# Windowed attention before a convolution: the probabilities become the stationary operand, and the weighted values are transposed back

## The reference

```python
def _L0_conv_ref(x, ac_w, ac_b, qkv_w, proj_w, proj_b):     # 16 heads of 8 channels, windows 8 x 8
    g = clip((x * ac_w + ac_b) * x, 0.0, 6.0)
    qkv = einsum('bchw,dc->bdhw', g, qkv_w)                   # cut into windows of 64 tokens
    attn = softmax(einsum('wnqd,wnkd->wnqk', q, k) * hd ** -0.5)
    o = einsum('wnqk,wnkd->wnqd', attn, v)
    return einsum('bchw,dc->bdhw', o, proj_w) + proj_b
...
x = x + _L0_conv_ref(_gn(x), ...)
x = x + _L1_conv_ref(_gn(x), ...)                             # 3 x 3 convolution, padding 1, plus bias
```

## Time and profile before

| | |
|---|---|
| median of 3 runs | 1495.81 us (1494.65 to 1499.69) |
| profiled execution: its time, its span | 1495.76 us, 1494.0 us |
| busy share TensorE, VectorE, ScalarE, GpSimd | 78%, 82%, 67%, 42% |
| mean granted clock of TensorE | 0.942 of full |
| DMA: moved, share of the engines' time | 144.93 MB, 29.6% for the kernel's queue |

### The profile page before, as it was taken

How to read it: one execution, slowest core, us unless ns; L and a number is a source line. 1 busy time by engine, 2 the same in 40 slices (tenths; PEclk the granted TensorE clock), 3 DMA queues, 4 the chain that set the end, 5 groups by cost and what they waited for, 6 DMA issues and landing times. The chain is left out here.

```text
span 1494.0 us, 56299 instructions
## 1 busy us (share of the span) xinstructions
PE 1171.3 (78%) x21860; PEld 696.7 (47%) x21860; DVE 1232.3 (82%) x1891; ACT 994.7 (67%) x1683; POOL 620.4 (42%) x438
## 2 busy tenths in 40 slices
PE   1288888988898986878747888988898898768875
PEld 1155555655565654333324555555565565423332
DVE  6678778887887985999985878887887888679998
ACT  2768777877787874544425877877787788644442
POOL 7124333433334432565632333333333334336665
PEclk9989999999999997899987999999999999979999
DMA  6143333333333330032324333333333343101111
GB/s 249 55 124 105 114 106 95 123 107 94 114 115 93 124 106 4 29 112 84 112 98 147 111 116 98 109 113 102 104 115 104 104 125 113 30 0 57 42 56 70
DMA packets 115466, 144.93 MB, mean 97 GB/s; under 512 B 21000, under 2 KB 91048, under 8 KB 114216
## 3 DMA queue, kind: packets, MB, share of 16 engines
q1 hardware_dynamic: 115240, 141.44, 29.6%
HBM read 72.16 MB, written 69.24 MB: 95 GB/s over the span
## 5 line engine op out<-in xcount | busy, mean ns | idle before, releaser
L503 ACT ACTIVATE work<-ps,ws 128x512 f32<-128x512 f32 x512 | 337.1, 682 | 61.8 <-PE ps L972 42.8
L734 DVE TENSOR_REDUCE m_all<-ps 128x8 f32<-128x512 f32 x512 | 328.1, 683 | 45.2 <-PE ps L949 44.0
L409 POOL TENSOR_TENSOR work<-work 128x512 f32<-128x512 f32 x128 | 162.7, 1271 | 370.4 <-ACT work L511 370.4
L415 POOL TENSOR_TENSOR g_lo<-work,g_hi 128x512 f16<-128x512 f32 x128 | 145.6, 1158 | 327.9 <-ACT g_hi L548 327.9
L960 PE MATMUL ps<-q_stack,k_stack 128*64 128x64 f16 x8192 | 216.4, 200 | 25.7 <-DMA q_stack<-max_scratch 24.0
L960 PEld LDWEIGHTS ps<-q_stack,k_stack 128*64 128x64 f16 x8192 | 179.4, 114 | 84.3 <-DMA q_stack<-max_scratch 45.4
L972 PE MATMUL ps<-work,v_ext 128*32 128x64 f32 x8192 | 210.1, 226 | 6.5 <-ACT work L503 0.6
L906 PE MATMUL ps<-work,c_hi 128*128 128x512 f16 x384 | 150.5, 392 | 69.6 <-DVE work L825 69.5
L601 ACT CAST work<-work 128x640 f16<-128x640 f32 x128 | 92.0, 720 | 145.6 <-DVE work L821 99.6
L949 PE MATMUL ps<-k_stack,q_stack 128*64 128x256 f16 x2048 | 177.8, 291 | 13.8 <-issue 4.8
L972 PEld LDWEIGHTS ps<-work,v_ext 128*32 128x32 f32 x8192 | 137.2, 110 | 92.0 <-issue 69.3
(11 more groups left out here) (130 smaller groups left out, 2022.9 us busy)
## 6 DMA issues: line engine op xcount, KB each, us to landing
stack_scratch<-work SPq DMA_DIRECT2D x128, 256.0 KB, 2.1
q_stack<-stack_scratch SPq DMA_DIRECT2D x64, 384.0 KB
k_stack<-stack_scratch SPq DMA_DIRECT2D x256, 96.0 KB
stack_scratch<-work SPq DMA_DIRECT2D x128, 128.0 KB, 2.1
out_dram<-work SPq DMA_DIRECT2D x32, 512.0 KB, 2.7
img<-in_x_dram SPq DMA_DIRECT2D x8, 1024.0 KB, 14.2
img<-in_x_dram SPq DMA_DIRECT2D x16, 512.0 KB, 3.9
q_stack<-zero_scratch SPq DMA_DIRECT2D x64, 32.0 KB
```

Source lines behind the costliest of these rows:

```text
L409: g.tensor_tensor(recip[h], sums[h], guess[h], ALU.mult).then_inc(near_done, 1)
L415: g.tensor_tensor(g_lo[:, m, :, e, :], g32.rearrange("p (w q) -> p w q", w=UW), g_hi[:, m, :, e, :], ALU.subtract).then_inc(g_lo_done, 1)
L503: a.activation(probs[:, w % 2, :], ps[:, ST_B + w % 2, :], ACT.Exp, scale=ws[:, R_EXP:R_EXP + 1]).then_inc(exp_done, 1)
L734: v.tensor_reduce(m_all[:, 0, 2 * h:2 * h + 2, p, :], ps[:, S_B + h, :].rearrange("p (g j k) -> p g j k", g=2, k=WIN), AX.X, ALU.max).then ...
```

## The change

The weighting is turned. `probs` holds a pair of windows (two halves of 512 columns), twice. `weigh(d, md, p)` takes 64 columns of `probs` as stationary operand and streams the 18 columns of `v_ext`: 16 values and 2 sums for a pair of heads. The output has tokens along partitions, so a sum stands beside its values; VectorE takes an ordinary reciprocal of 32 numbers a partition and multiplies with it (`divide`). `turn` transposes the result back on TensorE, `turned` copies it out on ScalarE, and `output` is one product instead of two. The shuffles, the guessed reciprocal and its Newton step fall away, with ScalarE's and GpSimd's part of them.

`g_hi` and `g_lo` are written once. `v_rows` writes the two head parities to the two halves of the partitions in 48 products of 64 columns instead of 24 of 128. The transposed maxima get a bank of their own (M_B) and rows 96 to 103 of `q_stack` are no longer filled with zeros from DRAM, since `scores` reads 96 rows.

The stages are shifted: a new stage E (unit i-1) holds the rest of D, and R works on unit i-2. The order on each engine is new. On TensorE a step is now: scores(0), weigh(n-1, 1), project(0), scores_t(n-1, 2), output(n-2), scores(1), weigh(n-1, 2), project(1), scores_t(n-1, 3), turn(n-1, 0), scores(2), weigh(n-1, 3), scores_t(n, 0), v_rows, scores(3), weigh(n, 0), scores_t(n, 1), turn(n-1, 1), transpose of the maxima. Maxima and exponentials stay one bank each. SyncE sends the maxima first, then q and k.

```diff
-VC = 4 * HD
+VC = 2 * HD + 2
...
-                return {s for s, lead in (("G", 4), ("H", 3), ("B", 2), ("C", 1), ("D", 0), ("R", -1), ("X", -2))
+                return {s for s, lead in (("G", 4), ("H", 3), ("B", 2), ("C", 1), ("D", 0), ("E", -1), ("R", -2))
...
+                    if "D" in on:
+                        after(sp, m_in, n - 1)
+                        after(sp, m_hi_done, n)
+                        after(sp, m_lo_done, n)
+                        sp.dma_start(maxd[m], m_pair[:, :, :]).then_inc(m_sent, 16)
+                        after(sp, m_sent, n)
+                        after(sp, st_done, n - BUFS)
+                        sp.dma_start(q_stack[ROWS:ROWS + MROWS, m, :, :].rearrange("r g (p t) -> r (g p) t", p=PAIRS),
+                                     maxd[m].rearrange("(a j) s t -> (j s) a t", j=HJ)).then_inc(m_in, 16)
                     if "B" in on:
...
+                        write(d, mb, 0)
+                        write(d, mb, 1)
                         after(sp, q_sent, d)
+                        after(sp, st_done, d - BUFS)
                         sp.dma_start(q_stack[0:ROWS, mb, :, :],
...
+                    def exps(d, p):
+
+                        after(act, pv_done, d, p - 1)
+                        for w in range(2):
+                            after(act, st_done, d, 2 * p + w + 1)
+                            a.activation(probs[:, p % 2, 512 * w:512 * w + 512], ps[:, ST_B + w, :], ACT.Exp,
+                                         scale=ws[:, R_EXP:R_EXP + 1]).then_inc(exp_done, 1)
...
+                    def turned(d, h):
+
+                        after(act, ot_done, d, h + 1)
+                        after(act, proj_done, d - 1)
+                        a.copy(o_t[:, 256 * h:256 * h + 256], ps[:, GA, 256 * h:256 * h + 256]).then_inc(ot_out, 1)
...
                     def divide(d, h):
 
...
+                        bank = ps[:, PV_B + h, 0:2 * HP * VC].rearrange("p (a c) -> p a c", c=VC)
+                        after(dve, pv_done, d, 2 * h + 2)
+                        v.reciprocal(rec[h], bank[:, :, 2 * HD:VC]).then_inc(rec_done, 1)
+                        after(dve, rec_done, d, h + 1)
+                        after(dve, ot_done, d - 1, h + 1)
+                        v.tensor_tensor(o_n[h].rearrange("p (a e d) -> p a e d", e=2, d=HD),
+                                        bank[:, :, 0:2 * HD].rearrange("p a (e d) -> p a e d", e=2),
+                                        rec[h].unsqueeze(3).broadcast_to([P, 2 * HP, 2, HD]), ALU.mult).then_inc(o_done, 1)
...
+                    def weigh(d, md, p):
+
+                        after(pe, exp_done, d, 2 * p + 2)
+                        if p == 0:
+                            after(pe, v_out, d)
+                        if p % 2 == 0:
+                            after(pe, o_done, d - 1, p // 2 + 1)
+                        if p == 2 and "D" in on:
+                            after(pe, m_lo_done, d + 1)
                         for hp in range(HP):
...
+                            col = (p % 2) * HP * VC + hp * VC
+                            for w in range(2):
+                                at = w * HP * WIN + hp * WIN
+                                mm = t_.matmul(ps[64 * w:64 * w + 64, PV_B + p // 2, col:col + VC],
+                                               probs[:, p % 2, at:at + WIN], v_ext[:, md, 2 * p + w, hp, :],
                                                start=True, stop=True)
...
+                    def turn(d, h):
+
+                        after(pe, o_done, d, h + 1)
+                        for a in range(2):
+                            mm = t_.transpose(ps[:, GA, h * 256 + a * P:h * 256 + a * P + P], o_n[h][:, a * P:a * P + P],
+                                              ident[:, :])
+                        mm.then_inc(ot_done, 1)
```

More of the change, by code:

```diff
@@ L124, in build @@
         qk = part(1536, 1024).bitcast(F16).rearrange("p (s t) -> p s t", s=4)
[L125 to L132, removed]
+        probs = part(2560, 2 * 1024).rearrange("p (s t) -> p s t", s=2)
+        rec = [part(4608 + 32 * h, 32).rearrange("p (a e) -> p a e", e=2) for h in range(2)]
+        o_n = [part(4672 + 256 * h, 256) for h in range(2)]
+        o_t = part(5184, 512)
+        res = part(5696, 512)
         cx = part(0, HALO * WIDE).rearrange("p (r c) -> p r c", r=HALO)
@@ L291, in one, with write @@
                     n = i + b * UNITS
+                    n_r = HD * PARTS
+                    def write(d, mb, which):
+                        lo, hi, into, sent = ((q_lo_done, q_hi_done, q_in, q_sent),
+                                              (k_lo_done, k_hi_done, k_in, k_sent))[which]
+                        after(sp, into, d - 1)
+                        after(sp, lo, d)
+                        after(sp, hi, d)
+                        to = stackd[mb, which]
+                        sp.dma_start(to[:, 0:2, :], qk[:, 2 * which:2 * which + 2, :]).then_inc(sent, 16)
+                        sp.dma_start(to[:, 2, :], qk[:, 1 + which, :]).then_inc(sent, 16)
@@ L403, in one @@
                     n = i + b * UNITS
[L405 to L409, removed]
+                    if "H" in on:
+                        after(pool, g_hi_done, n + 3)
+                        g.tensor_tensor(g_lo[:, m, :], g32, g_hi[:, m, :], ALU.subtract).then_inc(g_lo_done, 1)
                     if "R" in on:
[L411 to L420, removed]
+                        row, col = pixels(i - 2)
                         here = img[:, bass.ds(row, WS), bass.ds(col, UCOL)]
-                        after(pool, res_done, n - 1)
+                        after(pool, res_done, n - 2)
                         g.tensor_tensor(here, here, res.rearrange("p (r c) -> p r c", r=WS), ALU.add).then_inc(x1_done, 1)
@@ L884, in _ @@
             mm.then_inc(pe_step, 1)
[L885 to L886 removed]
+            mm = t_.transpose(ps[:, 1, 0:P], raw_proj, ident[:, :])
             mm.then_inc(pe_step, 1)
@@ L965, in weigh @@
-                    def weigh(w):
-                        after(pe, exp_done, n, w + 1)
-                        if w % 4 == 0:
-                            after(pe, o_done, n - 1, w // 4 + 1)
-                        for hp in range(HP):
-                            a, c = hp // 4, hp % 4
-                            col = (w % 4) * P + a * WIN
-                            mm = t_.matmul(ps[32 * c:32 * c + 32, PV_B + w // 4, col:col + WIN],
-                                           v_ext[:, m, w, hp, :], probs[:, w % 2, hp * WIN:(hp + 1) * WIN],
-                                           start=True, stop=True)
-                        mm.then_inc(pv_done, 1)
@@ new lines, in turn @@
+                    def turn(d, h):
[4 more added lines that the diff above has]
+                        mm.then_inc(ot_done, 1)
+                    def output(d):
+                        after(pe, ot_out, d)
+                        t_.matmul(ps[:, GB, :], pw[:, :], o_t, start=True, stop=True).then_inc(proj_done, 1)
```

381 lines of the change are left out of this document (152 added, 229 removed).

## The result

The changed kernel takes 1678.05 us (median of 4 runs, 1665.81 to 1682.24) against 1495.23 us: 1.1204 times the time before, interval 1.1138 to 1.1271. The forecast was slower, at 1560; the range ended at 1632.

The account below looks back on a forecast made before the run. The maxima's DRAM round trip plus queued work (14.7 us a unit) bounded the kernel; the keys' chain of 8.2 plus trip of 7.7 makes 15.9. With turn ends, 1494.0 + 64 + 1.8 = 1560 us, range 1450 to 1632.

Parts of the forecast that it names:

- The wait that goes: TensorE's wait for the maxima's 6.6 us DRAM round trip, claimed covered by about 9 us of other work.
- The wait that comes: First scores of each unit wait for the keys' DRAM round trip, some 2 us each time; chance 0.47.
- Its chain: Steps from the start of scores(0) to the keys' write leaving, stacked at 8.2 us.
- the trip: Keys' way through DRAM, from k's write to the next scores(0), taken at 7.7 us, between 6.9 and 8.6.
- W: Time of a pair's weighting block on TensorE, 16 matmuls with 32 weight loads: 0.88 us, bounds 0.36 and 1.76.
- the reciprocal: VectorE's reciprocal in divide(0), on the chain to the keys' write, taken at 0.2 us.
- the product: VectorE's product of 256 columns in divide(0), taken at 0.42 us.
- The step that failed: Half clock charged only to the first three blocks after a turn's end, about +1.6 us on the chain.
- the sum: Per image 7 x 17.4 + 7 x 17.5 + 17 x 15.9 = 514.6 us; +64 for two images.
- Rival B: TensorE slower: weight loads don't overlap (1638 us), or half clock at each unit's start (1609 us); chance 0.2.
- Rival C: Weight loads hide in the weighting, W = 0.36, so the kernel gets faster: 1475 or 1450 us; chance 0.28.

Follow-up runs that it names:

- e14: Changed kernel with weighting matmuls streaming up to 64 columns instead of 18 and two hardware-loop turns of twelve units: 1571.44 us, 1.0529 of the kernel before.
- e4: Changed kernel with eight f16 matmuls of 512 columns added behind each transpose of the maxima, filling TensorE's wait for the keys: 1588.58 us, ratio 1.0636.
- e1: Changed kernel without its DRAM loads into q_stack and k_stack after the first three units, writes kept: 1490.87 us, 0.9971 of the kernel before.
- e13: Changed kernel without DRAM loads into q_stack and k_stack after the first three units, weighting matmuls streaming up to 64 columns: 1447.97 us, ratio 0.9701.
- keys first: Changed kernel with both projections ahead of the first scores, q and k casts, remainders and writes moved up, output(n-2) moved back: 1592.59 us, ratio 1.06.

## Why the prediction was right in its direction and wrong in its size

**The wait that goes** was called rightly: no unit waits for the maxima's trip any more, and the work removed from VectorE, ScalarE and GpSimd was worth nothing by itself.

**The wait that comes** was called rightly, with its place: the first scores wait for the keys. Its chain was 8.2 us in the prediction and is 7.84 in the unit above; the trip was 7.7 and is 6.60 there, 7.9 in the middle of the changed kernel's units. The units of e14 with a chain of 7.8 to 7.9 take 14.4 to 15.6 us where 15.9 was stacked. No term was off by much: W, taken at 0.88, shows as 1.07 with the end of its last matmul (253.97), 1.0 to the next block's start, the reciprocal 0.35 instead of 0.2, the product 0.42.

The Trainium skill (TensorE: Matmul & The Clock Gate, LDWEIGHTS) says that a load takes its columns divided by 1.2 ns; in series that makes an estimate of 1.7 us for a block. The trace doesn't agree with loads in series: its rows give a load 161 ns in the mean, and 32 of them fit into 1.07 us, so they overlap.

**The step that failed** is the price of the clock: the sum charges half clock only in "In the unit after it the first three blocks run at half clock, about +1.6 on the chain", 7 units of 31, and leaves the clock full in the 17 units taken at 15.9. Rival B had the half clock in each unit, but again only at its start (1609 us), and with the remark that the idle stretch was shorter. Measured: a wait of 2.35 us, behind a lone transpose, is followed by the low clock, which can last far beyond three blocks; in the unit shown it lasts some 17 us of unbroken work, the keys' write leaves 11.86 us after the unit's first scores instead of 9.2 or 7.84, the unit takes 22.1 us, and then TensorE stops again. Each effect feeds the other, since the chain to the keys' write is almost all TensorE or waits for it.

Against the sum: the 17 other units of an image take 17.9 us in the mean where 15.9 was put, 66 us in two images; the unit at a turn's end and the one after it take 38.3 together where 34.9 was put, 48 us. These 114 us are nearly the whole miss of 118. The chain and trip of the prediction can't hold them, by these units of e14; how they divide between the low clock of the waits and that of the ends isn't measured unit by unit.

The Trainium skill (TensorE: Matmul & The Clock Gate, Part 1) says that the throttled state is the default and activity releases it. The trace of the changed kernel shows activity without release: busy in every window from 212 to 226 at 0.50.

**How the 183 us divide.** Four kernels form a square, in us:

| | stream of 18 | stream of up to 64 |
|---|---|---|
| with the trip | 1678 | 1622 |
| without it | 1491 | 1448 |

The trip costs 187 or 174 with all that its waits do to the clock, the short stream 56 or 43, nearly independent of it. By e4, 90 of the 187 come back when the wait is filled with work. What is left at the kernel's best inner period (13.6 against 14.7) is some 50 us of gain (48 inner units of 1.1 us) that the change does bring, and that the ends of the turns take back (this with the trip left out, e1).

**Rival C** (weight loads hide, W = 0.36) was wrong: W was above the taken value. **Rival B**'s first form, loads in series, was wrong too, though its 1638 us is the nearest number, by luck. Its second, the half clock in each unit, came nearest to what happens.

**Open.** Why a turn's end costs the changed order 7 us and more against 4 is shown only in part. The stop itself is 3.5 us in the end of e1 below and 4.0 in the earlier trace rows, the clock adds to it, and there is a second stop of 1.0 us in the middle of a weighting block, which the profile gives to nothing:

```profile
254.04 1.07 PE L878 MATMUL ps<-k_stack,q_stack 96*64 96x256 f16 x8 [3.52 <-issue]
254.89 1.21 PE L909 MATMUL ps<-v_ext,work 128*64 128x18 f32 x20
257.10 0.83 PE L909 MATMUL ps<-v_ext,work 128*64 128x18 f32 x12 [1.00 <-issue]
```

These rows are of e1, TensorE at 254 us. Why the wide stream shortens the stretches of low clock wasn't tried beyond the two widths, nor why the two images of e1 and e13 differ.

## What to carry to other kernels

When a change moves the period from one round trip through DRAM to another, stack the new chain from the first instruction that waits for the data to the write that sends the next; everything placed ahead of the producer counts, and what fits into the wait behind it is free (145 us against 2 for the same work, here). Then read the granted clock behind each new wait: here it doubled the loss, and adding columns or useless matmuls to the changed kernel made it 56 and 90 us faster. The same filling where there was no wait for the keys, on keys first, cost 10 us. And count the turns of a hardware loop: at 4 us an end, longer turns alone took the kernel before from 1495 to 1450.

## What the runs showed of the hardware that was not expected

- TensorE's granted clock fell to 0.50 after a wait of 2.35 us (behind a transpose of 0.33 us and 0.59 us of idling) and stayed there for some 17 us in which TensorE was busy without a gap. After another wait, of 2.52 us, with the same blocks behind it, it stood at 0.50 for some 3.4 us only.
- With up to 64 instead of 18 columns streamed a load in the weighting blocks, and no other edit, the stretches of low clock of 10 us or more fell from 20 to 8 (from 21 to 5 and from 14 to 4 in two other pairs).
- The same 32 loads and 16 float32 matmuls take 1.07 us whether a block streams 18 or up to 64 columns at full clock (237 against 227 ns for one matmul in the mean, over all clocks); at half clock 1.84 to 1.90.
